# Both edge sums of a graph kernel: a drain of TensorE behind each pair of products, tile work split over several pairs

## What is computed

```python
# first graph layer; edges sorted by dst, 100000 of them
h = x @ W
agg = segment_sum(edge_weight[:, None] * h[src], dst, 6250)
# ... batch norm over nodes, relu

# second graph layer
msg = edge_weight[:, None] * feat_in[src]
aggr = segment_sum(msg, dst, 6250) + (1.0 + eps) * feat_in
h = maximum(aggr @ W1 + b1, 0.0) @ W2 + b2
h = maximum(h, 0.0)
# ... layer norm of each row
```

## Time and profile before

| | us |
|---|---|
| median of 3 runs | 3917.03 |
| lowest and highest | 3912.73, 3925.56 |
| profiled execution, first to last instruction | 3891.6 |
| first edge sum, first gather to last gather issued | 370 to 1521 |
| its rest | to 1559 |
| second edge sum, first gather to last gather issued | 1952 to 3111 |
| its rest | to 3167 |
| mean granted TensorE clock (1 is full) | 0.819 |

### The profile page before, as it was taken

One profiled execution on the slowest core, in us unless ns is written; L12 is line 12 of the kernel. 1 busy time (PEld: TensorE's weight loads), 2 busy tenths in 40 slices (PEclk: granted clock), 3 DMA queues, 4 the chain that ended last, 5 costly groups with the idle time before them and its releaser, 6 DMA issues. The chain is left out here.

```text
span 3891.6 us, 55224 instructions
## 1 busy us (share of the span) xinstructions
PE 2650.3 (68%) x15016; PEld 2238.8 (58%) x15016; DVE 2586.9 (66%) x6599; ACT 1024.1 (26%) x2120; POOL 2179.1 (56%) x2145
## 2 busy tenths in 40 slices
PE   6886555444454545789946666666666657999998
PEld 4666343333343434689935444444444537999998
DVE  8997655444554555976746566666666677888886
ACT  0021000000000000567501111111111127888886
POOL 1434566666666664335456666666666603666665
PEclk8998777777777777899967777777887768999999
DMA  3011333333333332000133333333333334776775
GB/s 90 4 46 58 102 91 92 91 91 88 91 92 88 92 88 63 12 1 23 55 90 96 96 96 96 96 96 94 98 95 94 95 103 165 216 216 212 213 215 146
DMA packets 164219, 387.69 MB, mean 100 GB/s; under 512 B 46324, under 2 KB 95528, under 8 KB 150561
## 3 DMA queue, kind: packets, MB, share of 16 engines
q0 software_dynamic: 99072, 233.49, 22.0%
q1 hardware_dynamic: 64929, 151.65, 11.4%
HBM read 342.69 MB, written 42.97 MB: 99 GB/s over the span
## 5 line engine op out<-in xcount | busy, mean ns | idle before, releaser
L1089 POOL DMA_INDIRECT g_got<-table,e_source x1568 | 1493.5, 952 | 845.0 <-issue 440.0
L1115 DVE TENSOR_TENSOR A<-A,psum 128x256 f32 x1664 | 698.6, 420 | 876.3 <-remote 532.0
L1182 PE MATMUL psum<-g_got,g_route 128*128 x3328 | 1034.7, 473 | 141.0 <-DMA g_got<-table,e_source 74.2
L1182 PEld LDWEIGHTS psum<-g_got,g_route 128*128 128x128 f32 x3328 | 771.9, 241 | 329.0 <-issue 198.4
L786 PE MATMUL psum<-ident,g_rows 128*128 128x128 f32 x208 | 63.0, 401 | 663.3 <-ACT A L834 410.2
L1098 DVE TENSOR_SCALAR g_route<-columns,e_local,e_weight 128x128 f32<-128x128 f32 x1664 | 471.6, 362 | 17.4 <-issue 12.2
L786 PEld LDWEIGHTS psum<-ident,g_rows 128*128 128x128 f32 x208 | 29.7, 190 | 703.8 <-ACT A L834 505.7
L834 ACT COPY A<-psum 128x256 f32 x52 | 19.3, 372 | 999.4 <-issue 637.4
L369 POOL DMA_INDIRECT records<-rec,place x120 | 120.6, 1005 | 233.7 <-ACT rec L585 159.1
L140 PE MATMUL psum<-e_xt_hi,e_w_hi 128*128 128x256 f32 x832 | 238.2, 286 | 5.4 <-issue 5.2
L1612 POOL TENSOR_TENSOR f_ht_lo<-f_ht,f_ht_hi 128x512 fp32r<-128x512 f32 x100 | 134.2, 1347 | 181.1 <-ACT f_ht_hi L1551 174.6
(11 more groups left out here) (413 smaller groups left out, 5403.5 us busy)
## 6 DMA issues: line engine op xcount, KB each, us to landing
e_w<-in_m_w SPq DMA_DIRECT2D x104, 1024.0 KB, 5.1
g_got<-table,e_source POOLq DMA_INDIRECT x1568
expert_table<-g_normal SPq DMA_DIRECT2D x52, 128.0 KB
table<-xn SPq DMA_DIRECT2D x49, 128.0 KB
X<-in_x SPq DMA_DIRECT2D x1, 6144.0 KB
table<-f_ring SPq DMA_DIRECT2D x24, 256.0 KB, 2.1
out<-X SPq DMA_DIRECT2D x1, 6144.0 KB
f_w<-in_f_w SPq DMA_DIRECT2D x2, 1024.0 KB, 6.5
```

Of the source, the lines that this page charges most:

```text
L1089: pool.indirect_dma_start(got[:, c % RING, :], None, rows, bass.IndirectOffsetOnAxis(ap=source[:, c:c + 1].bitcast(U32), axis=0)).then_inc ...
L1115: dve.tensor_tensor(to, to, sums_of(c), ALU.add).then_inc(added, 1)
L1182: ins = pe.matmul(sums_of(c), route[:, c % (GB + GSEM), :], row(got, at[j % GSEM]), start=True, stop=True)
```

## The change

Four edits, all in the two edge sums:

1. `pe.drain()` behind every pair of products (832 slots, so 416 drains in each sum): TensorE's sequencer goes on only when all that TensorE was given is finished. A pair's share of tile work, if any, stands ahead of the drain.
2. The tile work is no longer given in one go behind a group but in pieces behind single pairs (there are eight pairs, 0 to 7, in a step). First sum: `turn` behind pair 3, one of the four products of `first_product` behind each of pairs 4 to 7. Second sum: `second_product` in halves behind pairs 0 and 1, `score` behind 2, `turn` behind 3, `first_product` in halves behind 5 and 6, `turn_normal` behind 7.
3. In the second sum each half of `second_product` has a drain of its own in front of it (102 more).
4. The bias of `second_product` is one product in a rounded float32 format (its high and low part as two rows against two rows of ones) in place of a plain float32 one. VectorE makes the two parts once, at the start of the second sum, after waiting for the parameters' loads.

```diff
-            def first_product(self, pe, k):
-                pe.wait_ge(self.loaded, 16)
-                pe.wait_ge(self.xt_out, k + 1)
-                for b in range(KD):
-                    for i in range(KD):
-                        ins = pe.matmul(psum[:, 7, D + b * P:D + (b + 1) * P], self.w[:, i, b * P:(b + 1) * P],
-                                        self.xt[:, i, :], start=i == 0, stop=i == KD - 1)
-                ins.then_inc(self.across, 1)
+            def first_product(self, pe, k, pieces=range(KD * KD)):
+                for piece in pieces:
+                    if piece == 0:
+                        pe.wait_ge(self.loaded, 16)
+                        pe.wait_ge(self.xt_out, k + 1)
+                    b, i = divmod(piece, KD)
+                    ins = pe.matmul(psum[:, 7, D + b * P:D + (b + 1) * P], self.w[:, i, b * P:(b + 1) * P],
+                                    self.xt[:, i, :], start=i == 0, stop=i == KD - 1)
+                    if piece == KD * KD - 1:
+                        ins.then_inc(self.across, 1)
...
-            def second_product(self, pe, k):
-                pe.wait_ge(self.hid_out, KD * k + KD)
-                for b in range(KD):
+            def second_product(self, pe, k, halves=range(KD)):
+                for b in halves:
+                    if b == 0:
+                        pe.wait_ge(self.hid_out, KD * k + KD)
                     pe.matmul(psum[:, 7, 0:D], self.hidden[:, b, :], self.w2[:, b, :], start=b == 0, stop=False)
-                pe.matmul(psum[:, 7, 0:D], ones[0:1, :], self.b2[:], start=False, stop=True).then_inc(self.made, 1)
+                    if b == KD - 1:
+                        pe.wait_ge(self.b2_ready, 2)
+                        pe.matmul(psum[:, 7, 0:D], self.ones_r[:], self.b2_parts[:], start=False, stop=True).then_inc(self.made, 1)
+
+            def make_bias_parts(self, dve):
+                dve.wait_ge(self.loaded, self.LOADS * 16)
+                s(dve.tensor_copy(self.b2_hi[:], self.b2[:]))
+                dve.tensor_copy(self.ones_r[:], ones[0:2, :]).then_inc(self.b2_ready, 1)
+                s(dve.tensor_tensor(self.b2_parts[:], self.b2[:], self.b2_hi[:], ALU.subtract))
+                dve.tensor_copy(self.b2_parts[0:1, :], self.b2_hi[0:1, :]).then_inc(self.b2_ready, 1)
...
+                    def between_pairs(n, pair):
+
+                        if n >= 1 and pair == 3:
+                            tiles_of.turn(pe, n - 1)
+                        if n >= 1 and pair >= GB // 2 - KD * KD:
+                            tiles_of.first_product(pe, n - 1, (pair - (GB // 2 - KD * KD),))
+
+                    def between_pairs_mlp(n, pair):
+
+                        if n >= 2 and pair in (0, 1):
+                            pe.drain()
+                            tiles_of.second_product(pe, n - 2, (pair,))
+                        if n >= 4 and pair == 2:
+                            tiles_of.score(pe, n - 4)
+                        if n >= 1 and pair == 3:
+                            tiles_of.turn(pe, n - 1)
+                        if n >= 1 and pair in (5, 6):
+                            tiles_of.first_product(pe, n - 1, (pair - 5,))
+                        if n >= 3 and pair == 7:
+                            tiles_of.turn_normal(pe, n - 3)
...
                                 if c % 2 == 1:
                                     ins.then_inc(pairs_summed, 1)
-                            if through_mlp and n >= 2 and g == 0:
-                                tiles_of.second_product(pe, n - 2)
-                            if through_mlp and n >= 4 and g == 0:
-                                tiles_of.score(pe, n - 4)
-                            if n >= 1 and g == 1:
-                                tiles_of.turn(pe, n - 1)
-                            if n >= 1 and g == (3 if through_mlp else 2):
-                                tiles_of.first_product(pe, n - 1)
-                            if through_mlp and n >= 3 and g == 3:
-                                tiles_of.turn_normal(pe, n - 3)
+                                    if through_mlp:
+                                        between_pairs_mlp(n, j // 2)
+                                    else:
+                                        between_pairs(n, j // 2)
+                                    pe.drain()
```

More of the change, by code:

```diff
@@ L853, in __init__ @@
                 self.w1, self.w2 = here("w1", [P, KD, D]), here("w2", [P, KD, D])
-                self.b1, self.b2 = here("b1", [P, KD]), here("b2", [1, D])
+                self.b1, self.b2 = here("b1", [P, KD]), here("b2", [2, D])
+                self.b2_hi, self.b2_parts, self.ones_r = here("b2_hi", [2, D], F32R), here("b2_parts", [2, D], F32R), here("ones_r", [2, P], F32R)
+                self.b2_ready = sem("g1_b2_ready")
                 self.scale, self.offset = here("scale", [P, D]), here("offset", [P, D])
@@ L868, in load @@
                 sp.dma_start(self.b1[:], g1_b1).then_inc(self.loaded, 16)
-                sp.dma_start(self.b2[:], g1_b2.rearrange("(a n) -> a n", a=1)).then_inc(self.loaded, 16)
+                sp.dma_start(self.b2[:], g1_b2.partition_broadcast(2)).then_inc(self.loaded, 16)
                 sp.dma_start(self.scale[:], g1_scale.partition_broadcast(P)).then_inc(self.loaded, 16)
@@ L880, in keep_turned, with first_product @@
                 act.copy(self.xt[:].rearrange("p k n -> p (k n)"), psum[:, 7, 0:D]).then_inc(self.xt_out, 1)
-            def first_product(self, pe, k):
-                pe.wait_ge(self.xt_out, k + 1)
-                for b in range(KD):
+            def first_product(self, pe, k, halves=range(KD)):
+                for b in halves:
+                    if b == 0:
+                        pe.wait_ge(self.xt_out, k + 1)
                     for i in range(KD):
@@ L887, in first_product @@
                                         self.xt[:, i, :], start=i == 0, stop=i == KD - 1)
-                ins.then_inc(self.hid, 1)
+                    if b == KD - 1:
+                        ins.then_inc(self.hid, 1)
             def hide(self, act, k):
@@ L1124, in _ @@
                     dve.engine_nop().then_inc(added, 1)
+                    if through_mlp:
+                        tiles_of.make_bias_parts(dve)
                     for n in range(STEPS):
```

## The result

The changed kernel took 4143.5 us (median of 4 runs, 4139.6 to 4146.2) against 3915.3 us of the kernel before beside it, a ratio of 1.0572, with 1.0556 to 1.0588 as its 95% interval. The forecast had been 3642 us, and the time lies outside the range of 3560 to 3930 us.

What follows compares the result with a forecast made beforehand. GpSimd's gathers were taken to bound both edge sums, with stalls from late counts. Gains of 131 + 18 and 115 + 11 us, together 275, took 3917 to 3642 us; own range 3567 to 3761, widened to 3560 to 3930.

Steps and rivals of the forecast that it cites:

- What bounds the kernel: Both edge sums: GpSimd's gathers bound them, 1.25 us for one, 980 us for all 784 in a sum.
- stalls of 171 and 179 us: First and second edge sum: time GpSimd stood still, put down to "remote" and TensorE's products.
- 25.4 us: Whole execution: time outside the profiled span, 3917.0 - 3891.6, taken to stay unchanged.
- A short run that is finished before more is given should be counted at once.: TensorE's pairs in both sums: drained short runs give counts in time, removing waits of about 8 us.
- whole gain of 275 us: Both sums: 131 and 115 us less stall, 18 and 11 us less behind the last gathers.
- The drained pair: TensorE in the edge sums: a pair with its drain takes 1.5 us at full clock, 2.3 at half.
- the drain waits where VectorE waited: Rival, both sums: drains sit out the late count, the step stays at 22 us; 3960 us, chance 0.10.
- DRAIN rows of several us: Sign in TensorE's queue that would show a drain that waits; no other size given.
- The rival of the clock: Rival, both sums: gaps behind drained pairs keep TensorE at half clock, steps 21 and 26 us; 4052 us, chance 0.13.
- Only the first sum gains: Rival: VectorE and the longer chain hold the second sum at 22.3 us a step; 3768 us, chance 0.13.
- Pieces and bias: Tile work and second sum's bias: covered waits cost nothing; bias product 0.38 us, 0 to 22 us gain taken as 0.
- the wait inside a piece: TensorE's tile work: waits hold following pairs and their drain, costed at nothing; about 1 us a step without cover.

Runs made afterwards that it cites:

- e6: Kernel before, unchanged, run again where counts come in time: 3510.0 us, sums of 983.8 and 991.1 us.
- e17: Kernel before with plain transfers for the first sum's gathers, pieces and rounded bias without drains in the second; counts late: 3533.9 against 3910.6 us, ratio 0.9042.
- e7: Kernel before with one slot's product made fifteen times in every step, holding TensorE; counts late: 4133.6 us, ratio 1.0539.
- e8: Changed kernel with one slot's product made fifteen times in every step; counts late: 4844.5 us, ratio 1.2346 to the kernel before.
- e5: Changed kernel, run again where counts come in time: 3511.8 against 3510.0 us for the kernel before, ratio 1.0012.
- e15: Kernel before with one-pass bfloat16 products in the first sum, only a drain behind each pair in the second; counts late: 3989.0 against 3911.3 us, ratio 1.0194.
- e9: Kernel before with 1200 further small transfers from SyncE's queue in the first sum, adding semaphore increments; counts late: ratio 1.0016.
- e16: Same kernel as e17, run where counts come in time: 3320.6 against 3505.5 us for the kernel before, ratio 0.9468.

## Why the prediction was wrong, point by point

*What bounds the kernel.* Right, and the runs with counts in time show it better than the earlier trace rows could: 1.25 us a gather, 983.8 and 991.1 us for 784 of them. The stalls of 171 and 179 us were real in that trace, but e6 has almost none of them with the same program. The reading went wrong in taking them for a property of the kernel. A hint stood in the rows: "remote", 386.2 us of it, which means here that the count's record stands far behind the end of any product that makes it. Another stood in the trace: it holds 20135 updates of semaphores, e6's trace of the same kernel 45494. The 25.4 us that the sum carried as time outside the span were not that: in the changed kernel's profiled execution it is 4139.6 - 4137.7 = 1.9 us, and the rest is the distance between two executions of the kernel before. It cancels in the forecast of 3642 us.

What was late had a shape that I did not read. The first sum of before has 361 of its 416 counts on record; 45 times six of them stand some 60 ns apart, in the earlier trace rows at 1016.11 to 1016.41 for the six pairs from 1002.78 to 1008.12. The last of the six comes 7.4 us behind its product's modelled end and the first 11.9 us (medians). So it was not that single counts took 8 us: all counts of a run were held and let go together.

*"A short run that is finished before more is given should be counted at once."* This is the step that failed, and the whole gain of 275 us hung on it. It rested on the earlier trace rows: no lateness behind the last gather. But the 24 records that are counted in time there are as long a run as the late ones, so what had stopped was the gathers alone. Nothing in the rows showed a short run beside gathers, and I took it that such a run would be counted in time. It is not: in the changed kernel each pair is a run of its own, finished before more is given, and still 81 of the 416 drains of the first sum are late, by 3.8 us in the mean. The other way round, e17's first sum has ten runs of six to ten pairs without a pause and no gathers, and no count of it is late. So the length of the run was not a condition, and the gathers were.

*The drained pair.* Forecast 1.5 us at full clock and 2.3 at half. In the changed kernel's timeline pairs start at 1006.50, 1007.84 and 1009.66, so 1.34 and 1.82 us, the second with the read of ring places: 1.58 us in the mean. The size at full clock was right; where counts come in time it costs nothing, since it is hidden under GpSimd (ratio 1.0012 for the change, 1.0007 for the drains alone).

*The rival "the drain waits where VectorE waited".* This is what happened, with a chance of 0.10 and a price of 3960 us, and the sign that I had named for it, DRAIN rows of several us, is the one that came. The mechanism was right, as the drains of the two sums up to the last gather show (count, then shortest, median and longest ns):

```profile
L1228 PEldq DRAIN  x398: 892/1972/10875, 391.2 to 1598.9; - x199
...
L1228 PEldq DRAIN  x399: 665/1968/10393, 2046.9 to 3353.6; - x200
```

The price was short by 184 us. It held that the step stays at 22 us because the late count was already waited for, and added only the drains' own time. But the wait changed its owner. VectorE's wait lay beside TensorE's further pairs; the drain's lies in TensorE's queue, in front of them, and adds to TensorE's step (e7 against e8: 1.0 against 6.3 us of the same stall). The sum should have been TensorE's: eight drained pairs of 1.58 us, 1.4 of the tile's work and 5.9 of lateness are 19.9 us by themselves, against 1232.5/52 = 23.7 us measured. The 3.8 us between them are left for the part at half clock and the waits for routes and sums; no run separates these two.

By the Trainium skill's page "PSUM — Partial Sum Buffer", section "Engine vs sequencer instructions", a drain waits until the engine is fully idle. The prediction weighed this rule against the rows and gave it only this rival; the runs agree in both kinds: a drain ends 0.04 us behind the modelled end of the last product where counts come in time (mean of e5's first sum), and not before the late count where they don't (5.16 us long in the timeline above).

*The rival of the clock.* It is not what decided, and its size stays open. The windows of both sums, first those of the kernel before, then those of the changed one (clock behind the five busy times):

```profile
370.00:1521.00 1151.00, 563.66 (x2156) 452.32 (x2154) 588.27 (x1724) 55.95 (x146) 742.61 (x784) 0.73 0.32 92
1952.00:3111.00 1159.00, 750.81 (x2664) 556.94 (x2664) 722.72 (x2275) 122.97 (x430) 749.72 (x784) 0.77 0.33 95
```
```profile
370.00:1603.00 1233.00, 730.28 (x2131) 505.92 (x2131) 594.97 (x1725) 55.96 (x146) 744.41 (x784) 0.69 0.30 86
2038.00:3355.00 1317.00, 871.63 (x2598) 580.98 (x2599) 727.46 (x2277) 131.93 (x430) 749.29 (x784) 0.70 0.29 84
```

Where counts are late the clock falls from 0.73 to 0.69 and from 0.77 to 0.70; in the timeline above TensorE stands idle behind a long drain and goes on at half. Drains don't bring it down where counts come in time (0.80 and 0.80, 0.83 and 0.86), and drains without the pieces don't in the late kind either (e15's second sum, 0.78). Since TensorE's step is the bound of the changed kernel where counts are late, a lower clock should cost something there; how much was not measured, and it may be part of the 52 us left open. *Only the first sum gains* didn't occur.

*Pieces and bias.* Right: 0 us (ratios 1.0005 and 1.0003 where counts come in time; +5 us in e17's second sum, within the spread). The bias product takes 0.38 us (median of e5), as forecast from the earlier trace rows. That the wait inside a piece holds the following pairs and costs little by itself holds where no drain stands between; with late drains it may be part of the 52 us left open.

## What to carry to other kernels

Before a drain is put in to make a signal prompt, find out which engine would wait for the signal and what else that engine could do meanwhile: a late count costs what lies behind the waiting instruction, and a drain puts the producer's whole queue there. Where a fault is gone in one place of a trace, look which of its supposed conditions really stopped there; the others are not shown. Where a trace puts long waits down to "remote" and lacks updates that the program must have made, profile the kernel again on another occasion before changing it; here 400 of 3915 us, and the whole reason for the change, belonged to the occasion. To price a fix for a wait that isn't understood, first take away one suspected condition at a time: plain transfers in place of gathers told more than the change itself.

## What the runs showed of the hardware that I had not expected

- The same kernel took 3502 to 3511 us in some groups of runs and 3911 to 3922 us in others, 11% more, once on the same chip. In the longer ones TensorE's increments of semaphores arrive late while GpSimd's gathers are in flight. They come in bunches: in the first sum of before 45 times six counts stand some 60 ns apart, 7.4 us (median) behind the last product; in e9's, where the counts are as late, 44 times. A drain ends late there too, by up to 9.0 us in the changed kernel, so it is not VectorE's view of the counts alone that is late. Other stages show little of it: between the sums and behind them the trace of before is 25 and 27 us longer than e6's.
- In these executions, and in the same stretches, records of updates are missing. From the first product to the last the first sum of before has 3600 of them against 14783 in e6; e17's first sum, where no gathers run and nothing is late, has 14284, as many as e16's, and its second 3930 against 16597. The Trainium skill's page "NOTIFIC — the notification-queue block", section "Overflow: three behaviours, one of which stalls the engine", has a mode in which a full ring of records stalls the producer, and another that drops records; further on, in the section on the overflow path, the page says that the runtime uses the one that drops. Missing records fit that, and no run here shows what holds the counts: whether the records are held up by what delays them or are its cause, and what sets the condition, stays open.
- A drain of TensorE is cheap where counts come in time and TensorE is not the bound: it ends 0.04 us behind the modelled end of the last product (mean of the 416 drains of e5's first sum), and the kernel with 832 of them alone shows no loss (ratio 1.0007, 0.9997 to 1.0016).
- The granted clock was 0.97 in the sum with plain transfers (e17, TensorE busy 485 of 756 us) and 0.56 in the one with one-pass products (e15, busy 313 of 1147 us), which took 1146.3 us against 1150.8 all the same.
